# Three fp16 products for half of the value steps of a cross-attention kernel, with the context preparation moved later

## The reference, cut to what matters

```python
xn, ln = layernorm(x), layernorm(latents)          # context 1601x128, latents 64x128
q, k, v = heads(ln @ Wq) * scale, heads(kv[..., :INNER]), heads(kv[..., INNER:])  # kv = concat(xn, ln) @ Wkv
sim = where(mask, q @ k.T, -max)                   # 16 heads, 64 x (1601 + 64)
out = softmax(sim) @ v                             # this product: the "values" of the kernel
x1 = layernorm(out @ Wout) + latents ...           # then ALiBi self-attention, then the FFN
```

## Time and profile before

| what | value |
|---|---|
| median of 3 runs | 900.16 us |
| the profiled execution's own time | 900.01 us |
| its span, first to last instruction | 898.0 us |
| mean granted TensorE clock | 0.963 of full speed |
| TensorE matmul busy | 832.3 us (93%) |
| VectorE busy | 594.8 us (66%) |
| ScalarE busy | 450.5 us (50%) |
| GpSimd busy | 186.5 us (21%) |

### The profile page before, as it was taken

One profiled execution on the slowest core, in us unless ns is written; L12 is line 12 of the kernel. 1 busy time (PEld: TensorE's weight loads), 2 busy tenths in 40 slices (PEclk: granted clock), 3 DMA queues, 4 the chain that ended last, 5 costly groups with the idle time before them and its releaser, 6 DMA issues.

```text
span 898.0 us, 20741 instructions
## 1 busy us (share of the span) xinstructions
PE 832.3 (93%) x6742; PEld 445.9 (50%) x6743; DVE 594.8 (66%) x1515; ACT 450.5 (50%) x757; POOL 186.5 (21%) x354
## 2 busy tenths in 40 slices
PE   5699999999999999999999999999999999999753
PEld 4344544545454555545454545545454645455522
DVE  5777666666657576766657566766666576747577
ACT  5365454546465545546464545545465554443242
POOL 3011021212122221212222221211222222212101
PEclk9799999999999999999999999999999999999655
DMA  6113221111212121111212111201212111110001
GB/s 204 34 41 103 80 56 40 37 55 52 58 40 54 51 55 54 46 29 52 58 40 55 50 55 55 55 20 52 58 41 59 49 53 53 40 41 17 4 1 47
DMA packets 98347, 45.82 MB, mean 51 GB/s; under 512 B 72100, under 2 KB 90376, under 8 KB 98184
## 3 DMA queue, kind: packets, MB, share of 16 engines
q1 hardware_dynamic: 98256, 45.34, 18.2%
q10 hardware_dynamic: 56, 0.05, 0.0%
HBM read 25.69 MB, written 3.26 MB: 32 GB/s over the span
## 4 chain that ended last, share of the span: by engine, by line
PE 71%; DVE 17%; issue 6%; ACT 3%; DMA 1%; DVEq 1%; POOL 1%; ACTq 0%; SPq 0%; POOLq 0%
PE bank L1299 20%; PE bank L1353 7%; PE bank L1272 6%; PE bank L1227 5%; PE bank L1274 4%; PE bank L1276 4%; DVE mx L1694 4%; PE bank L1244 4%; PE bank L1370 3%; PE bank L1414 3%; DVE xf_all L1723 3%; PE bank L1389 2%; PE bank L1399 2%; PE bank L1243 2%; ACT arena L971 1%
## 5 line engine op out<-in xcount | busy, mean ns | idle before, releaser
L986 ACT ACTIVATE p<-bank,maskbias 128x512 f32<-128x512 f32 x224 | 154.2, 688 | 232.6 <-PE bank L1276 231.1
L1299 PE MATMUL bank<-p,xv 128*128 128x512 f32 (+1 forms) x512 | 238.0, 616 | 0.3 <-POOL arena L840 0.3
L1694 DVE TENSOR_REDUCE mx<-bank 128x1 f32<-128x512 f32 x256 | 165.5, 682 | 53.2 <-PE bank L1244 52.8
L1690 DVE TENSOR_TENSOR qkl_l<-bank,qkl_h 128x512 f16<-128x512 f32 x64 | 41.1, 685 | 76.7 <-ACT qkl_h L974 76.7
L1299 PEld LDWEIGHTS bank<-p,xv 128*128 128x128 f32 (+1 forms) x512 | 74.9, 188 | 31.5 <-issue 23.8
L1272 PE MATMUL bank<-qkc_h,xtT_h 128*128 128x512 f16 (+1 forms) x256 | 86.9, 389 | 0.0
L1244 PE MATMUL bank<-xtT_h,qkc_h 128*128 128x448 f16 x256 | 86.7, 358 | 0.0
L1274 PE MATMUL bank<-qkc_l,xtT_h 128*128 128x512 f16 (+1 forms) x256 | 85.0, 379 | 0.0
L1276 PE MATMUL bank<-qkc_h,xtT_l 128*128 128x512 f16 (+1 forms) x256 | 85.0, 379 | 0.0
L1243 PEld LDWEIGHTS bank<-ltT,qkl_h 128*128 128x128 f16 x256 | 24.9, 97 | 95.4 <-DVE mx L1694 53.9
L1353 PE MATMUL bank<-arena,wvF 128*64 128x128 f32 x1024 | 69.3, 278 | 0.0
(11 more groups left out here) (260 smaller groups left out, 1461.1 us busy)
## 6 DMA issues: line engine op xcount, KB each, us to landing
arena<-den_dram SPq DMA_DIRECT2D x62, 128.0 KB, 3.2
qkc_h<-arena SPq DMA_DIRECT2D x30, 256.0 KB, 2.4
qkc_l<-arena SPq DMA_DIRECT2D x30, 256.0 KB, 2.4
raw<-in_ctx SPq DMA_DIRECT2D x32, 192.0 KB, 2.5
raw<-in_ctx SPq DMA_DIRECT2D x64, 32.0 KB, 2.2
lt<-lt_dram SPq DMA_DIRECT2D x60, 31.8 KB, 2.1
arena<-in_L_xattn_Wkv SPq DMA_DIRECT2D x1, 1024.0 KB, 6.7
ltT_dram<-x_all SPq DMA_DIRECT2D x4, 256.0 KB, 3.5
```

Of the source, the lines that this page charges most:

```text
L986: a.activation(p32[0:r, slot, :], sbank[t % SRING][0:r, :], ACT.Exp, bias=bias).then_inc(s_probs_ready, 1)
L1299: op = mm(bk[:, :], rows_of[at, :], p32[at, slot, :], start=tile < 2, stop=tile in (0, plan.TILES - 1))
L1694: v.tensor_reduce(mx[:, hq_tile, part:part + 1], bk[:, 0:width], AX.X, ALU.max).then_inc(s_jobs_taken, 1)
```

## The change

It does these things:

- `SPLIT` lists the steps whose value product is made in fp16 halves: steps 0 and 1 of both batches of a pair (the paired steps), and steps 4 to 7 of the even batch, 8 of 16 steps. For these `probs` makes the exp twice, once as fp16 and once as fp32; GpSimd subtracts the one from the other (`low_probs`, one step later in its order); and `values` waits for this low half and makes three fp16 products in place of one fp32 product.
- The value rows of these steps are split in the same way: latents once at the start (`latents_first` on ScalarE, `latents_low` on GpSimd, stored and loaded as fp16 pairs), context rows in GpSimd's `prep`.
- The places move: STATS and AGGR from t=4 to 5, RSTD from 4 to 6, XHAT and MASK from 6 to 8 (which is t=0 of the next batch), T from s=0 to s=1 (odd batch) and from s=7.5 to s=9 (even batch), RDEN of the even batch from t=3 to 5 of the odd one, MOVE from s=8 to s=11. In SyncE's queue the shift rows go ahead of the denominators' rows when k=1.

```diff
-WINDOW = Plan(N - 448, dict(
-    STATS={4: (0, 4)}, AGGR=4, RSTD=4, XHAT=6, MASK=6,
+WINDOW = Plan(N - 448, ({0, 1, 3, 4}, {0, 1}), dict(
+    STATS={5: (0, 4)}, AGGR=5, RSTD=6, XHAT=8, MASK=8,
...
-    ODD=dict(T=[0], MAX=[2.5, 3, 3, 3.5, 4, 4, 4.5, 5], MT=6),
+    ODD=dict(T=[1], MAX=[2.5, 3, 3, 3.5, 4, 4, 4.5, 5], MT=6),
     NEXT=dict(QP=[0, 0.5], QC=[1.5, 6.5], QL=[8.5, 9.5]),
-    EVEN=dict(T=[7.5], MAX=[10.5, 11, 11, 11.5, 12, 12, 12.5, 13], MT=14), XV={2: (0, 4)},
-    RDEN=3, MOVE=8, ST1=[3, 4, 5, 6], YN=[6, 7], XB=7, ST2=8, M0=9, P0=9, X1=10, X1B=15, M1=10, P1=10,
+    EVEN=dict(T=[9], MAX=[10.5, 11, 11, 11.5, 12, 12, 12.5, 13], MT=14), XV={2: (0, 4)},
+    RDEN=(3, 5), MOVE=11, ST1=[3, 4, 5, 6], YN=[6, 7], XB=7, ST2=8, M0=9, P0=9, X1=10, X1B=15, M1=10, P1=10,
...
-        lt_dram = nc.dram_tensor("lt_dram", [TOK, D], F32).ap()
+        lt_dram = nc.dram_tensor("lt_dram", [TOK, 2 * D], F16).ap()
...
+        p_all = words(11264, 2, HALF)
+        p_halves = p32[:, :, :].rearrange("p a b -> p (a b)").bitcast(F16).rearrange("p (a h b) -> p a h b", a=RING, h=2)
...
# SyncE, in the loop over k
-                        if since or k == 1:
+                        if since and k == 0:
                             rden_rows(b - 1, 1 - par, pair)
-                        if since and k == 0:
                             load_x(i - 1)
+                        if more and k == 1:
+                            load_rows(plan, i, last, 1 - par)
+                        if k == 1:
+                            rden_rows(b - 1, 1 - par, pair)
...
-                        if more:
+                        if k == 0:
                             load_rows(plan, i, last, 1 - par)
...
# GpSimd
+            def low_probs(plan, i, k, t):
+
+                if (k, t) in plan.SPLIT:
+                    r, slot, made = plan.rows(t), slot_of(plan, k, t), plan.halves_made(i, k, t)
+                    pool.wait_ge(s_probs_ready, (i * 2 + k) * plan.STEPS + t + 1)
+                    g.tensor_tensor(p_halves[0:r, slot, 1, :], p_all[0:r, (plan.halves_made(0, k, t) - 1) % 2, :], p_halves[0:r, slot, 0, :], ALU.subtract).then_inc(s_p_lo, 1)
...
-                    op = g.tensor_copy(xv[:, par, c0:c1, 0:127], raw[:, par, c0:c1, 0:127])
+                    if first < c1:
+                        g.tensor_copy(xv_halves[:, par, first:c1, 0, 0:127], raw[:, par, first:c1, 0:127]).then_inc(s_xv_hi[par], 1)
+                    if first > c0:
+                        op = g.tensor_copy(xv[:, par, c0:first, 0:127], raw[:, par, c0:first, 0:127])
+                    if first < c1:
+                        pool.wait_ge(s_xv_hi[par], (n - par) // 2 + 1 if isinstance(n, int) else (n - par + 2) // 2)
+                        op = g.tensor_tensor(xv_halves[:, par, first:c1, 1, 0:127], raw[:, par, first:c1, 0:127], xv_halves[:, par, first:c1, 0, 0:127], ALU.subtract)
...
                     for s in range(2 * plan.STEPS):
                         k, t = divmod(s, plan.STEPS)
+                        if t > 0:
+                            low_probs(plan, i, k, t - 1)
+                        elif since or k == 1:
+                            low_probs(plan, i - 1 + k, 1 - k, plan.STEPS - 1)
                         if not (last and k == 1):
+                            ahead(plan, i * 2 + k + 1, 1 - k, t + plan.STEPS)
                             prep(plan, i * 2 + k + 1, 1 - k, t)
...
# ScalarE, probs
-                a.activation(p32[0:r, slot, :], sbank[t % SRING][0:r, :], ACT.Exp, bias=bias).then_inc(s_probs_ready, 1)
+                if (k, t) in plan.SPLIT:
+                    made = plan.halves_made(i, k, t)
+                    a.activation(p_halves[0:r, slot, 0, :], sbank[t % SRING][0:r, :], ACT.Exp, bias=bias)
+                    if happened(made - 2):
+                        act.wait_ge(s_p_lo, made - 2)
+                    a.activation(p_all[0:r, (plan.halves_made(0, k, t) - 1) % 2, :], sbank[t % SRING][0:r, :], ACT.Exp, bias=bias).then_inc(s_probs_ready, 1)
+                else:
+                    a.activation(p32[0:r, slot, :], sbank[t % SRING][0:r, :], ACT.Exp, bias=bias).then_inc(s_probs_ready, 1)
...
# TensorE, values
-                pe.wait_ge(s_probs_ready, b * plan.STEPS + t + 1)
+                split = (k, t) in plan.SPLIT
+                if split:
+                    pe.wait_ge(s_p_lo, plan.halves_made(i, k, t))
+                else:
+                    pe.wait_ge(s_probs_ready, b * plan.STEPS + t + 1)
...
-                for bk, at in parts:
-                    op = mm(bk[:, :], rows_of[at, :], p32[at, slot, :], start=tile < 2, stop=tile in (0, plan.TILES - 1))
+                if split:
+                    halves_of = lt[:, k, :, :] if tile == 0 else xv_halves[:, k, c, :, :]
+                    for n, (row, prob) in enumerate(((1, 0), (0, 0), (0, 1))):
+                        for bk, at in parts:
+                            op = mm(bk[:, :], halves_of[at, row, :], p_halves[at, slot, prob, :], start=tile < 2 and n == 0, stop=last and n == 2)
+                else:
+                    for bk, at in parts:
+                        op = mm(bk[:, :], xv[at, k, c, :], p32[at, slot, :], start=tile < 2, stop=last)
...
# VectorE
+                        if more:
+                            ahead(plan, b + 1, 1 - k, t + plan.STEPS)
                         prep(plan, i, last, s - 0.5)
                         prep(plan, i, last, s)
```

More of the change, by code:

```diff
@@ L64, with __init__ @@
 class Plan:
-    def __init__(self, first, at):
+    def __init__(self, first, split, at):
         self.own = False
@@ L87, in __init__ @@
         self.STEPS = len(self.steps)
+        self.SPLIT = [(k, t) for k in range(2) for t in range(self.STEPS) if self.steps[t][0] in split[k]]
+        assert len(self.SPLIT) % 2 == 0
         self.GROUPS = -(-self.CH // 4)
@@ L137, in rows, with halves_made, split_chunks @@
         return P if half is None or tile > 1 else (M, self.TAIL)[tile]
+    def halves_made(self, i, k, t):
+        return i * len(self.SPLIT) + self.SPLIT.index((k, t)) + 1
+    def split_chunks(self, k):
+        return [c for c in range(self.CH) for t in range(self.STEPS) if self.steps[t][0] > 0 and self.chunk(self.steps[t][0]) == c and (k, t) in self.SPLIT and self.steps[t][1] in (None, 0)]
     def chunk(self, tile):
         return self.CH - 1 if tile == 1 else tile - 2
-WHOLE = Plan(0, dict(
+WHOLE = Plan(0, ({0}, {0}), dict(
     STATS={14: (0, 5), 15: (5, 9), 16: (9, 13)}, AGGR=17, RSTD=18, XHAT=20, MASK=21,
@@ L329, in program @@
         s_xtT_hi = es.enter_context(nc.semaphore("xtT_hi"))
+        s_xv_hi = [es.enter_context(nc.semaphore(f"xv_hi{k}")) for k in range(2)]
+        s_p_lo = es.enter_context(nc.semaphore("p_lo"))
+        s_lat_hi = es.enter_context(nc.semaphore("lat_hi"))
+        s_lat_lo = es.enter_context(nc.semaphore("lat_lo"))
+        s_lt_loaded = [es.enter_context(nc.semaphore(f"lt_loaded{k}")) for k in range(2)]
         s_xv_ready = es.enter_context(nc.semaphore("xv_ready"))
@@ L680, in attention @@
                     sp.dma_start(aw[:, k, :], w).then_inc(s_in_aw, 16)
+                store_block(0)
+                for par in range(2):
+                    for half in range(2):
+                        sp.dma_start(lt[M * half:M * half + M, par, :, :].rearrange("p h d -> p (h d)"),
+                                     lat_halves[M * par:M * par + M, 0, :, :].rearrange("p h d -> p (h d)")).then_inc(s_lt_loaded[par], 16)
                 load_rows(plan, None, False, 0)
@@ L851, in attention @@
             def attention(plan):
+                for k in range(2):
+                    for c in range(plan.CH):
+                        if c in plan.split_chunks(k):
+                            g.memset(xv_halves[:, k, c, 0, 127:128], 1.0)
+                            g.memset(xv_halves[:, k, c, 1, 127:128], 0.0)
+                        else:
+                            g.memset(xv[:, k, c, 127:128], 1.0)
                 pool.wait_ge(s_mask_made, 1)
-                for t in range(plan.STEPS):
+                for t in range(2 * plan.STEPS):
                     ahead(plan, 0, 0, t)
@@ L857, in attention @@
                     ahead(plan, 1, 1, t)
+                    if t == plan.LAT:
+                        latents_low(0)
                 def body(i, since, last):
@@ L938, in late_weights @@
                     a.activation(sig[:, :], clip_row[:, :], ACT.Exp, scale=-1.0).then_inc(s_sig_e, 1)
+                for j, (_, centre, _) in BLOCK_AT.items():
+                    if s == centre + 1:
+                        latents_first(j)
                 for kind, k in late_at(s):
@@ L1456, in attention @@
                 for t in range(plan.STEPS - LAG, plan.STEPS):
-                    values(plan, B - 1, 1, t)
+                    values(plan, PAIRS - 1, 1, t)
                 pe.wait_ge(s_probs_ready, B * plan.STEPS)
@@ L1811, in attention @@
                 setup(plan)
```

(2 more changed lines are left out.)

72 lines of the change are left out of this document (42 added, 30 removed).

## The result

The changed kernel takes 1001.53 us (median of 4 runs, 996.53 to 1004.28) against 900.16 us: ratio 1.1125, 95% interval 1.1073 to 1.1177. It is slower, as forecast, but by 101 us and not by 20; the measured time lies far outside the stated range. The profiled execution took 1003.12 us.

What follows compares the result with a forecast made beforehand. PE's work was taken as the bound (49.02 of 50.05 us per pair). Per pair -1.68 + 1.11 + 1.52 + 0.45 = +1.40 us, in all +19.8 on 900.0: 920 us, own range 905 to 933, 8 in 10 884 to 934.

Steps and rivals of the forecast that it cites:

- SyncE's queue: DMA order in SyncE's queue: shift rows ahead of the denominators' rows at k=1, costed at nothing.
- The sum: All terms together: +1.40 us per pair, -1.23 in the last pair, +19.8 us in all, giving 920 us.
- QC0: PE's wait at this two-bank job for T of the odd batch, behind both exps of step 1: 1.32 us.
- QL1: PE's wait at this two-bank job for T of the even batch, with step 9 split too: 1.52 us.
- values of step 6: PE's wait for GpSimd's low half, made only after SHIFT: 0.45 us, between 0.33 and 1.18.
- The products: Value steps on PE: three fp16 passes for four save 0.21 us each, 1.68 us per pair over 8 steps.
- rival D: Paired value steps: their fp16 products run one after the other, 28 us more, 948 us; chance 0.03.
- The small terms: A spared MAX wait and longer waits for VectorE behind QC0: zero together, 0.3 us either way; latents' loads and MOVE zero.
- The MAX wait: PE's 0.31 us before a MAX job, which VectorE may spare without STATS and RDEN in its way.
- Rival C: GpSimd subtractions hold back VectorE's XHAT or line 1751, 1.09 us a pair reaching PE: 937 us; chance 0.08.
- The 33 us: Extra by the skill's port rule, if subtractions meeting normalisation or residual sums held PE back twice a pair.
- Rivals A and B: A: QC0 and QL1 waits covered, 877 us, chance 0.22; B: both about half covered, 898 us, chance 0.11.

Runs made afterwards that it cites:

- e4: The kernel before with only RDEN and MOVE late and SyncE's changed order, fp32 products and old context places: 942.78 us, ratio 1.0485.
- e2: The changed kernel with the context places (STATS, AGGR, RSTD, XHAT, MASK, T) back as before, the late query load left in: 940.33 us.
- e3: The changed kernel with the query load ahead of the denominators' rows and the context places back as before: 894.36 us, ratio 0.9938.
- e1: The changed kernel with the next pair's query load issued ahead of the denominators' rows in SyncE's queue: 923.69 us, ratio 1.0271.
- e7: e1 with the jobs' high halves (T's included) made between the two exps of a split step on ScalarE: 907.86 us, ratio 1.0094.
- e5: e3 with GpSimd's low half of step 6 made at the end of its step 6, ahead of SHIFT: 884.71 us, ratio 0.9843.
- e8: The kernel before with only the context places late as in the change, fp32 products and single exps: 914.52 us, ratio 1.0173.
- e10: The kernel before with context places, RDEN, MOVE and SyncE's order all as changed, fp32 products and single exps: 991.92 us, ratio 1.104.
- e9: e6 with steps 2 and 3 of the even batch split too, ten of sixteen steps in fp16 products: 877.62 us, ratio 0.9759.
- e6: e5 with the high halves of T and QP0 made between the two exps of a split step: 880.37 us, ratio 0.9797.

## Why the prediction was right in its sign and wrong in its size

**The step that failed** is "SyncE's queue: ... the shift rows go ahead of the denominators' rows at k=1, and I cost both at nothing, because the denominators are used in the next pair". It asked who needs the moved transfers, and not what stands behind them. Behind them in the in-order queue is the load of the next pair's queries, which PE needs 3.8 us after the last shift row was issued (426.99 for the row, QP0 at 430.79). The move puts a store with a wait for its own landing and two loads in front of it. Nor was this among the rivals, whose costliest gave 948 us. In the kernel before, SyncE's own timeline shows the tight place (the query load issued at 428.23, T and QP at 430.3 to 430.8), and the prediction has no row of it. The runs give for it: 43.3 us by itself (e4), 46.0 between e2 and e3, 77.8 between the changed kernel and e1. The first is smaller because T stands ahead of QP0 there, and the shift rows leave 0.5 us sooner. The sum had no term for a lower clock either, and that is 31 of the 78 us; it comes only with this wait.

**The three waits** were right, in place, cause and size. QC0: 1.32 forecast, 1.35 measured; QL1: 1.52 and 1.56; values of step 6: 0.45 and 0.39. The second exp's part in the first two (0.59) was measured with 0.57 and 0.58 (e7), SHIFT's part in the third by its removal (e5). With the query load repaired the kernel takes 923.69 us where the sum gave 920 (e1). A steady pair of e1 takes 51.36 us (416.19 to 467.55), where 51.45 was forecast. That these two agree to 0.1 us is in part luck, as two errors of half a microsecond cancel: PE's busy time falls by 2.25 us in it (49.02 to 46.77) and not by 1.68, and its idle time rises by 3.56 us (1.03 to 4.59) and not by 3.08. And outside the steady pairs the sum missed some 6 us: from the first MT job to the third e1 takes 51.30 us and the kernel before 44.15, 7.1 us more where 1.4 were forecast. PE waits there 3.5 us for VectorE ahead of the transposes of line 1199 (0.7 before, line 1121) and 1.7 us for a subtraction. In e8 and e10, which have no fp16 products, the same stretch takes 45.6 and 45.2 us, so the loss comes with the products; with which part of them no run takes apart.

The stated range does not follow from its own terms: 0.75 us down and 1.03 us up per pair give some 908 to 936 us, not 905 to 933. The measured time is outside both.

**The products** save more than forecast, and the 0.21 us is not the same at each place. In the timeline of PE of the kernel after, a full value step and a paired one, each with what follows it:

```profile
401.99 0.81 PE L1386 MATMUL bank<-p,xv 128*128 128x512 f16 x3
402.74 0.28 PE L1304 MATMUL bank<-arena,wk_h 64*128 64x128 f16 x4
...
417.09 0.82 PE L1386 MATMUL bank<-p,lt 64*128 64x512 f16 x6
417.84 0.20 PE L1320 MATMUL bank<-ltT,qkl_h 128*128 128x64 f16 x1
```

The same full step, with the same neighbours, took in the kernel before

```profile
400.39 1.02 PE L1299 MATMUL bank<-p,xv 128*128 128x512 f32 x2
401.35 0.28 PE L1227 MATMUL bank<-arena,wk_h 64*128 64x128 f16 x4
```

0.96 us, and takes 0.75: 0.21 us less, as forecast. But this is one place of several. The same product of step 6 took 1.06 us (406.29 to 407.35) and takes 0.75 (407.50 to 408.25), and a step of 0.86 us, like the one from which the forecast was worked out, saves only 0.13 (e9, step 2). The paired step takes 0.75 in place of 1.06 us: 0.31 us less where 0.21 was forecast. So the products of the two row halves overlap, and rival D falls.

Where the waits are taken away, most of the gain arrives: e6 is 2% faster than the kernel before. A steady pair of it takes 48.46 us, 1.59 less than before: PE is busy for 1.99 us less (47.03 in place of 49.02), and its idle time is 0.40 us longer. The first pair takes 4.4 us more than before (48.55 and 44.15 us from the first MT job to the third), which takes a part of it back.

**The small terms.** The MAX wait of 0.31 us that might have gone is still there, and behind QC0 there is now one of 0.48 us for QC0's low half, where PE stood idle for 0.18 us before. The growth is the 0.31 us that the value step ahead of it is shorter by; the forecast had 0.21 for it and set it to zero:

```profile
423.44 0.20 PE L1320 MATMUL bank<-ltT,qkl_h 128*128 128x64 f16 x1 [0.31 <-DVE mx L1784]
...
447.20 0.20 PE L1320 MATMUL bank<-ltT,qkl_h 128*128 128x64 f16 x1 [0.48 <-DVE arena L1776]
```

No wait of PE is put down to the latents' loads or to MOVE. The start does have new waits, as said above.

**Rival C, GpSimd against VectorE.** Its mechanism is seen and its price was nothing. The normalisation takes 555 ns in the mean in the changed kernel (median 342, longest 1265) and 557 in e1, but 335 in e3, where the same subtractions run and XHAT is at another place, and 346 in e10, with XHAT late and no subtractions. Only both together lengthen it. In one pair its four instructions take 3.04 us from 406.27, beside subtractions at 406.28 and 407.81; T comes at 412.21 and waits for nothing there. The Trainium skill's rule (SBUF — State Buffer, section "Who interferes with whom") agrees with these rows. The forecast's other place for it, the residual sum of line 1751 at s=10 (line 1841 after), is lengthened too, from 351 to 1054 ns in the median. The 33 us that I worked out beside the rule did not come: in the loop no wait of PE is put down to either.

**Rivals A and B** fall: PE stood at QC0 and QL1 in each of 15 pairs.

## What to carry to other kernels

When an item moves in an in-order queue, list what stands behind its new place and when each of those is needed; that the moved item itself is not urgent says nothing about them. Above all move no item that waits for its own completion (here a store and its read-back) in front of the tightest load. In a kernel whose bound engine has no idle time, a job that must be finished before the next one may start should stand a full step ahead of it, and a second pass on the engine that hands it over (here the second exp) lengthens the wait by its own length. And a long wait of TensorE is to be priced with slow work behind it. When a total agrees with its forecast, compare the busy and the idle time of the bound engine with their own terms: here two errors of half a microsecond a pair stood behind an agreement of 0.1 us.

## What the runs showed of the hardware

- The granted clock halves after waits of PE of 3.4 us and more (1.00, then 0.65 and 0.50 in stretches of 2 us, and 1.00 again after about 4 us). In e4, with waits of about 2.4 us, it falls in some pairs and in others not (0.50 from 406 to 408 us, 1.00 from 458 to 462, behind waits of 2.35 and 2.43 us); in e1, with waits of at most 2.1 us at QC0 and QL1, the loop keeps 1.00 in each stretch of 100 us from 100 to 800 us. With the lower clock the same PE work takes 31 us longer (828.7 against 797.4 us busy, changed kernel and e1), 19 us (822.8 against 803.9, e2 and e3) and 13 us (845.5 against 832.3, e4 and before), beside waits for lq of 51, 35 and 34 us.
- Six fp16 matmuls of 512 columns on 64 rows each take 0.75 us from start to start, as long as three on 128 rows: the two halves of the rows work at the same time. In fp32 a full step takes 0.86, 0.96 or 1.06 us by what stands around it, in fp16 mostly 0.73 to 0.76.
- A GpSimd subtraction of 128x512 (fp32 minus fp16 into fp16) takes 1.16 us, more than half of the 128x1024 fp32 one with 1.90 us.
